# Selective scan: the input term dt·x·B made by TensorE in PSUM, decays in SBUF, D·x added by VectorE

## The chip, the cores and the metric

The kernel runs on one core of a Trainium2 chip. The metric is the device time of one launch in microseconds (us); smaller is better. A core has five engines that matter here: TensorE (PE; its weight loads are listed apart, as PEld), VectorE (DVE), ScalarE (ACT), GpSimd (POOL) and SyncE (SP, which issues the DMAs). Each runs its own list of instructions in order and waits on counting semaphores.

## The reference, cut to what matters

The kernel is a small network of several layers: a Mamba block (norm, input projection, convolution, selective scan, output projection), a layer of experts, a second mixer, and a gated feed-forward layer. The change lies in the selective scan of the first block. For each of 4 sequences of 256 tokens, 1024 channels d and 16 states n it computes

```python
def step(h, inp):                      # h: [batch, d, n], one step per token
    x_t, dt_t, B_t, C_t = inp
    dA = jnp.exp(dt_t[..., None] * A)                              # decay
    dBx = dt_t[..., None] * B_t[:, None, :] * x_t[..., None]       # input term
    h = dA * h + dBx
    y = jnp.einsum('bdn,bn->bd', h, C_t)
    return (h, y)
# and afterwards  y = y + x * D
```

## The kernel before

The stages run one behind the other, each in a block of its own that starts when all engines have left the one before. Three concern us. `scan_front` makes x (tile `xc`), dt and the rows of B and C (`sp_bcn`, 64 rows of 1024 tokens); it writes B and C to DRAM as `bc_rows`, and ends with VectorE adding the two parts of dt (L530). `selective_scan` is the stage that is changed. `scan_out_proj` multiplies the result by the output weights. Later, the norm stage `n1_` loads x again and then the weights of the experts, both from SP's queue.

In `selective_scan` channels lie on the 128 partitions (8 tiles of 128) and tokens along the row. The work is cut into 8 blocks, one for each pair of channel tiles (PR = 4) in each half of the tokens (HALF = 512, so 2 sequences); a block is a row of 2 x 512 = 1024 elements per partition. Each block has 16 units, one for each state n: 128 units in all. The `half` loop is a Python loop, the loop over the pairs is a hardware loop (`Fori`) on each engine. A unit is:

- ScalarE makes the decay exp(A·dt) into PSUM, two instructions of 510 columns (L657, tile `ss_da`, two buffers). The first token of each sequence has decay zero, so one scan can run over several sequences.
- The input term `ss_dbx` = u·B, with u = dt·x (L709, in PSUM) and B's row broadcast over the partitions (`ss_bc`), is one product of 1024 elements: on VectorE for three states of four (L703), on GpSimd for the fourth (L752, `ss_dbp`, from a copy `ss_us` of u in SBUF that ScalarE makes, L665).
- VectorE scans: h = decay·h + input (L726, out to one of four slices of tile `o`).
- GpSimd multiplies h by the broadcast row of C (L757, `ss_pr`, two buffers).
- TensorE adds that product into PSUM, `ss_y`: two f32 matmuls of 512 columns with the identity as weights (L775). At a block's start it has put D·x there, with the diagonal of D as weights (L768, `ss_dg` made by ScalarE at L669).
- At a block's end ScalarE copies `ss_y` over `xc` (L680).

The order on VectorE is: input term of unit n+1, then scan of unit n. TensorE waits for GpSimd's product, GpSimd for VectorE's scan, and ScalarE's next decay for the scan that frees its buffer:

```python
if n + 1 < NST:
    if not by_pool(n + 1):
        inputs(k, n + 1)
```

Of the kernel before, what the change touches and what calls it, by code (L numbers as in the profile page):

```python
# [21 lines left out]
P = 128  # L22
# [60 lines left out]
def build(nc, I, out):  # L83

    with ExitStack() as top:
        sems = {}

        def sem(name):
            if name not in sems:
                sems[name] = top.enter_context(nc.semaphore(name))  # L90
            return sems[name]

# [11 lines left out]
        bc_dram = nc.dram_tensor("bc_rows", [2 * NST, TOK], F32, kind="Internal").ap()  # L104
# [12 lines left out]
        def norm_stage(tag, x, o, load_x, xT, rms, keep, weights=None):  # L117
# [3 lines left out]
            with scope() as c:  # L121
# [24 lines left out]

                with nc.Block() as block:
# [126 lines left out]
                    def _(pe):  # L274
                        if xT is None:
                            return
                        for m in range(MT):
# [3 lines left out]
                            i.then_inc(s_t, 1)  # L281

# [14 lines left out]
        with scope() as c0:  # L297
            o = sb(c0, "o1", [P, MT, DM])
            with scope() as c1:
                xc = sb(c1, "xc", [P, CD, TOK])  # L300
                sz = sb(c1, "sz", [P, CD, TOK])
                with scope() as cdt:
                    dt = sb(cdt, "dt", [P, CD, TOK])
                    with scope() as c2:
# [4 lines left out]
                        scan_front(nc, sem, sb, banks, I, xT, xc, sz, dt, cst, eps, bc_dram, o)  # L309
                    selective_scan(nc, sem, sb, banks, I, xc, dt, o, ident, bc_dram)  # L310
# [25 lines left out]
def scan_front(nc, sem, sb, banks, I, xT, xc, sz, dt, cst, eps, bc_dram, o):  # L336
# [5 lines left out]
    with ExitStack() as c:  # L342
# [23 lines left out]
        s_sd, s_bcn, s_out = sem("sp_sd"), sem("sp_normed"), sem("sp_bc_out")  # L366
# [9 lines left out]
        with nc.Block() as block:  # L376
            @block.sync
            def _(sp):
# [13 lines left out]
                sp.dma_start(bc_dram, bcn[RNK:R, :]).then_inc(s_out, 16)  # L392
# [14 lines left out]
            def _(pe):  # L407
# [59 lines left out]
                for i in range(done, NT):  # L467
                    steps(i)

            @block.vector  # L470
            def _(dve):
# [59 lines left out]
                dve.wait_ge(s_dt, CD)  # L531
# [40 lines left out]
def selective_scan(nc, sem, sb, banks, I, xc, dt, o, ident, bc_dram):  # L572

    DA, RH = 2, 4
    PR = CD // 2
    W = 2 * HALF
    with ExitStack() as c:
        bcb = sb(c, "ss_bc", [P, 2 * NST, HALF])
        al = sb(c, "ss_al", [P, CD, NST])
        na = sb(c, "ss_na", [P, CD, NST])  # L580
        dd = sb(c, "ss_d", [P, CD])
        dg = sb(c, "ss_dg", [P, 2, P])
        dbx = [sb(c, f"ss_dbx{i}", [P, 2, HALF]) for i in range(2)]
        us = sb(c, "ss_us", [P, 2, HALF])
        dbp = [sb(c, f"ss_dbp{i}", [P, 2, HALF]) for i in range(2)]
        hv = o[:].rearrange("p (i m) d -> p i (m d)", i=RH)
        hh = [hv[:, i, :] for i in range(RH)]
        pr = [sb(c, f"ss_pr{i}", [P, 2, HALF]) for i in range(2)]
        wide = lambda name: c.enter_context(nc.psum_tensor(name, [P, W], F32))
        da = [wide(f"ss_da{i}") for i in range(DA)]  # L590
        u, yb = wide("ss_u"), wide("ss_y")
        s_in = sem("ss_in")
        s_bc = [sem(f"ss_bc_in{i}") for i in range(NST // 4)]
        s_a, s_z, s_da, s_u, s_dbx, s_h = (sem("ss_a"), sem("ss_zero"), sem("ss_decay"), sem("ss_u_ready"),
                                           sem("ss_dbx_ready"), sem("ss_h_ready"))
        s_pr, s_y, s_dg, s_fin = sem("ss_prod"), sem("ss_summed"), sem("ss_diag"), sem("ss_done")
        s_us, s_dbp = sem("ss_u_copied"), sem("ss_dbx_by_pool")
        UH = PR * NST
        BR = 4
        NV = NST // BR * (BR - 1)  # L600
        NP = NST // BR
        two = lambda t: t.rearrange("p (a t) -> p a t", a=2)

        def row(n):
            return bcb[:, n, :].unsqueeze(1).to_broadcast([P, 2, HALF])

        def by_pool(n):
            return n % BR == BR - 1

        def v_count(n):  # L610
            return n // BR * (BR - 1) + n % BR

        def rows_landed(eng, half, n):

            if n % BR == 0:
                eng.wait_ge(s_bc[n // BR], 32 * (half + 1))

        def tiles(eng, body):

            with eng.Fori(0, PR - 1) as k:  # L620
                body(k, False)
            body(PR - 1, True)

        with nc.Block() as block:
            @block.sync
            def _(sp):
                sp.dma_start(al[:], I["a_log0"]).then_inc(s_in, 16)
                sp.dma_start(dd[:], I["d_0"]).then_inc(s_in, 16)
                for half in range(NH):
                    for r0 in range(0, NST, BR):  # L630
                        if half:
                            sp.wait_ge(s_dbx, PR * NV - NV + v_count(r0 + BR))
                            sp.wait_ge(s_dbp, PR * NP - NP + (r0 + BR) // BR)
                        for r in (r0, NST + r0):
                            if half and r >= NST:
                                sp.wait_ge(s_pr, RH + UH - NST + r0 + BR)
                            src = bc_dram[r:r + BR, half * HALF:(half + 1) * HALF]
                            sp.dma_start(bcb[:, r:r + BR, :], src.partition_broadcast(P)).then_inc(s_bc[r0 // BR], 16)

            @block.scalar  # L640
            def _(act):
                act.wait_ge(s_in, 32)
                act.activation(al[:], al[:], ACT.Exp).then_inc(s_a, 1)
                act.wait_ge(s_a, 1)
                act.activation(na[:], al[:], ACT.Copy, scale=-1.0).then_inc(s_a, 1)
                act.wait_ge(s_a, 2)
                act.wait_ge(s_z, DA)
                for half in range(NH):
# [1609 lines left out]
```

## Time and profile before

| | |
|---|---|
| median of 3 runs | 2677.43 us |
| lowest, highest | 2675.04, 2677.46 us |
| span of the profiled execution | 2670.2 us |
| TensorE busy | 2308.2 us (86%) |
| VectorE busy | 1957.9 us (73%) |
| ScalarE busy | 1460.8 us (55%) |
| GpSimd busy | 1238.2 us (46%) |

The profile is of one execution. Times in it are counted from the start of its span. The span leaves out what lies around the instructions (about 7 us here). The profile gives for each engine the busy share in 40 slices of the span, groups of equal instructions with their mean duration, the idle time before them and what ended it, and a timeline. Matmuls overlap each other, so the duration of one (592 ns) is longer than the distance from one start to the next; for TensorE it is the distance between starts that counts. An f32 matmul appears as two MATMUL records, each with its weight load (2 x 128 x 2 = 512 records on L775).

### The profile page before, as it was taken

The page shows a single profiled execution, that of the slowest core. Times are in us where ns is not written, and L with a number is a line of the kernel's source. Part 1 is how long each engine was busy: PE and PEld are TensorE (multiplying, and loading weights), DVE is VectorE, ACT ScalarE, POOL GpSimd, SP SyncE. Part 2 cuts the span into 40 slices and gives each one's busy share as a digit, 9 for nine tenths or more (in the row PEclk, how much of TensorE's full clock was granted, in tenths as well). Part 3 has the DMA queues.
Part 4 walks back from the last instruction along what each step waited for, and adds up shares of the span by engine and source line. Part 5 has one row for each costly group of instructions (what it writes and reads, how often), then busy time and mean ns, then how long its engine had stood idle before and what let it go on. Part 6 is the DMA issues. An engine that isn't in the chain of part 4 may idle for free. (4 is left out here: it accounts for less than half of the span.)

```text
span 2670.2 us, 33973 instructions
## 1 busy us (share of the span) xinstructions
PE 2308.2 (86%) x11172; PEld 1672.4 (63%) x11172; DVE 1957.9 (73%) x3153; ACT 1460.8 (55%) x3092; POOL 1238.2 (46%) x788
## 2 busy tenths in 40 slices
PE   5966676667454999999999999999999999779997
PEld 4532222225434677777777777777777777569996
DVE  4559989994554786686685776775866866688777
ACT  2344444443103796685785866866956857742221
POOL 2119988993101464363462553644643624542212
PEclk9989998998576999999999999999999999899999
DMA  2030030000112232231332322322312312211010
GB/s 80 26 115 13 0 126 0 0 0 32 60 36 74 90 119 66 76 115 52 90 99 57 101 76 71 111 72 74 108 67 77 113 52 88 91 45 37 36 48 32
DMA packets 113218, 175.20 MB, mean 66 GB/s; under 512 B 9696, under 2 KB 77664, under 8 KB 112032
## 3 DMA queue, kind: packets, MB, share of 16 engines
q1 hardware_dynamic: 113056, 173.16, 20.6%
q8 instruction: 87, 1.43, 0.2%
q14 instruction: 75, 0.61, 0.1%
HBM read 166.71 MB, written 6.42 MB: 65 GB/s over the span
## 5 line engine op out<-in xcount | busy, mean ns | idle before, releaser
L78 PE MATMUL mg_pb<-xTh,mg_wh 128*128 128x512 f32 x1152 | 479.2, 416 | 16.9 <-POOL mg_wl L1233 16.9
L1243 POOL TENSOR_TENSOR mg_y<-mg_hT,mg_sg 128x512 f32<-128x512 f32 x128 | 187.7, 1466 | 598.9 <-DVE mg_hT L1479 598.9
L79 PE MATMUL mg_pb<-xTl,mg_wh 128*128 128x512 f32 x1152 | 454.3, 394 | 0.0
L80 PE MATMUL mg_pb<-xTh,mg_wl 128*128 128x512 f32 x1152 | 452.1, 392 | 0.0
L775 PE MATMUL ss_y<-ss_pr,cst 128*128 128x512 f32 x512 | 278.5, 678 | 125.7 <-POOL ss_pr L757 125.4
L1427 DVE SCALAR_TENSOR_TENSOR mg_hT<-mg_pb,mg_cw,mg_hT 128x510 f32<-128x510 f32 (+2 forms) x432 | 318.4, 741 | 31.6 <-ACT mg_hT L1599 22.8
L757 POOL TENSOR_TENSOR ss_pr<-o,ss_bc 128x1024 f32<-128x1024 f32 x128 | 301.9, 2374 | 45.9 <-DVE o L726 26.9
L1454 DVE TENSOR_TENSOR mg_m<-mg_gb,mg_cb 128x384 f32<-128x384 f32 x512 | 265.3, 549 | 71.6 <-ACT mg_gb L1649 68.2
L775 PEld LDWEIGHTS ss_y<-ss_pr,cst 128*128 128x128 f32 x512 | 98.4, 210 | 305.6 <-POOL ss_pr L757 225.8
L657 ACT ACTIVATE ss_da<-dt,ss_na 128x510 f32 (+1 forms) x256 | 165.9, 680 | 208.0 <-DVE o L726 208.0
L78 PEld LDWEIGHTS mg_pb<-xTh,mg_wh 128*128 128x128 f32 x1152 | 217.2, 189 | 76.5 <-issue 19.2
L80 PEld LDWEIGHTS mg_pb<-xTh,mg_wl 128*128 128x128 f32 x1152 | 217.3, 189 | 51.1
L79 PEld LDWEIGHTS mg_pb<-xTl,mg_wh 128*128 128x128 f32 x1152 | 217.9, 189 | 38.4
L1649 ACT ACTIVATE mg_gb<-mg_nd 128x256 f32<-128x256 f32 x512 | 189.6, 370 | 54.4 <-DVE mg_nd L1472 54.4
L726 DVE TENSOR_TENSOR_SCAN o<-ss_da,ss_dbx 128x1024 f32<-128x1024 f32 x96 | 215.6, 2273 | 0.0
L1643 ACT ACTIVATE mg_gb<-mg_abc,mg_tabs 128x128 f32<-128x128 f32 x512 | 183.0, 357 | 23.1 <-DVE mg_m L1454 22.1
L1233 POOL TENSOR_TENSOR mg_wl<-mg_ws,mg_wh 128x1024 fp32r<-128x1024 f32 x72 | 177.5, 2465 | 6.0
L78 PE MATMUL mg_tb<-mg_wogh,mg_yh 128*128 128x512 f32 x448 | 179.9, 401 | 0.0
L80 PE MATMUL mg_tb<-mg_wogh,mg_yl 128*128 128x512 f32 x448 | 177.0, 395 | 0.0
L79 PE MATMUL mg_tb<-mg_wogl,mg_yh 128*128 128x512 f32 x448 | 176.9, 395 | 0.0
L1329 PE MATMUL mg_py<-mg_m,mg_hc 128*64 128x256 f32 x1024 | 166.1, 403 | 9.6 <-DVE mg_m L1454 9.5
L1503 DVE SCALAR_TENSOR_TENSOR o<-mg_tb,mg_rs,o 128x512 f32<-128x512 f32 x56 | 41.8, 746 | 179.7 <-PE mg_tb L80 179.7
(289 smaller groups left out, 5217.4 us busy)
## 6 DMA issues: line engine op xcount, KB each, us to landing
mg_abc<-acs_rows SPq DMA_DIRECT2D x256, 256.0 KB, 3.4
mg_ws<-in_w_in SPq DMA_DIRECT2D x72, 512.0 KB, 3.8
ss_bc<-bc_rows SPq DMA_DIRECT2D x16, 1024.0 KB, 6.4
mg_wos<-in_w_out SPq DMA_DIRECT2D x64, 256.0 KB, 3.6
ff_ws<-in_w SPq DMA_DIRECT2D x7, 1024.0 KB, 4.7
x<-in_x SPq DMA_DIRECT2D x16, 256.0 KB, 4.1
ip_ws<-in_w_in SPq DMA_DIRECT2D x8, 512.0 KB, 3.6
ff_w2s<-in_w SPq DMA_DIRECT2D x7, 512.0 KB, 5.7
```

The costliest lines, as they stand in the source:

```text
L78: pe.matmul(out, lhs[0], rhs[0], start=start, stop=False)
L79: pe.matmul(out, lhs[0], rhs[1], start=False, stop=False)
L80: return pe.matmul(out, lhs[1], rhs[0], start=False, stop=stop)
L726: dve.tensor_tensor_scan(hh[n % RH], da[n % DA][:], src[:].rearrange("p a t -> p (a t)"), 0.0, ALU.mult, ALU.add).then_inc(s_h, 1)
L757: pool.tensor_tensor(pr[n % 2][:], two(hh[n % RH]), row(NST + n), ALU.mult).then_inc(s_pr, 1)
L775: i = pe.matmul(yb[:, a * HALF:(a + 1) * HALF], ident, pr[n % 2][:, a, :], start=False, stop=n == NST - 1)
L1233: pool.tensor_tensor(wl[s % 2][:], ws[:], wh[s % 2][:].bitcast(F32), ALU.subtract).then_inc(s_lo, 1)
L1243: pool.tensor_tensor(yb[:, p % RING, t], hT[s % 2][:, t], sg[s % 2][:, t], ALU.mult).then_inc(s_y2, 1)
L1427: i = dve.scalar_tensor_tensor(out=d3, in0=s3, scalar=w[:, TAPS - 1 - k:TAPS - k], in1=d3, op0=ALU.mult, op1=ALU.add)
L1454: dve.tensor_tensor(mm[u % 4][:], gb[u % 2][:, 0:BLK], cbt[:, u // 2, :], ALU.mult).then_inc(s_m, 1)
L1643: act.activation(gb[u % 2][:, 2 * P:BLK], abc[(BATCH * p + b) % 3][:, hh, P:SEQ], ACT.Exp, bias=tabs[g % 2][:, 2, 2 * b, 2 * q + hh:2 * q ...
L1649: act.activation(gb[u % 2][:, 0:2 * P], nd[u % 4][:], ACT.Exp, scale=1.0 if by_dve(p, b) else -1.0).then_inc(s_e, 1)
```

## The change

The input term moves from VectorE and GpSimd to TensorE. For a matmul that gives u[d, t]·B[t, n] with channels on the output partitions, u is turned: per block TensorE transposes the eight 128x128 pieces of u into PSUM (`turn`), ScalarE copies them to SBUF as `ss_uT` (`copied`), and then per unit TensorE runs eight f32 matmuls of 128x128 by 128 columns (`inputs`): weights are a piece of `ss_uT`, the moving operand is a diagonal matrix of B for that state and those 128 tokens (`ss_diag`). The result goes to `ss_dbx`, now in PSUM with two buffers; the decays go to SBUF. The diagonals are made once per half: for the first by VectorE (states 0 to 3), GpSimd (4 to 9) and ScalarE (10 to 15), for the second by ScalarE during the last block of the first half. For this `scan_front` turns the B rows with eight transposes and a copy into a small tile `bt`, ahead of VectorE's last additions. Only C's rows go through DRAM and are broadcast.

u is made in SBUF by VectorE. The D·x term is no longer a matmul: at the end of a block VectorE computes xc = D·xc + sum (`skip`, two instructions of 512). PSUM tile `z` (two buffers) holds first the turned u and then the block's sum. `ss_pr` has three buffers instead of two. All loops over blocks are unrolled. TensorE's order in step i is: input term of unit i+2, then (after unit 8 of a block) the turn for the next block, then the sum of unit i-2.

Since the unrolled waits need no offsets but semaphores run short, `n1_` clears the semaphores of the three stages on SP between its load of x and its load of weights, for use again.

```diff
+                        if tag == "n1_":
+                            cleared.extend(clear_stages(sp, "ip_", "sp_", "ss_"))
...
+                for m in range(MT):
+                    i = pe.transpose(pq[:, m * R:(m + 1) * R], bcn[:, m * P:(m + 1) * P], cst[0:R, C_ID:C_ID + R])
+                i.then_inc(s_bt, 1)
...
+                dve.wait_ge(s_bt, 1)
+                dve.tensor_copy(bt[:], pq[:].rearrange("p (m r) -> p m r", r=R)[:, :, RNK:RNK + NST]).then_inc(s_dt, 1)
...
+    RH, RP, LEAD, LAG = 4, 3, 2, 2
+    TURN_AT, EVAC_AT = 8, 4
...
+                def decay(i):
+                    kk, n = divmod(i, NST)
+                    if i >= 2:
+                        act.wait_ge(s_h, i - 1)
+                    for a in range(2):
...
+                        ins = act.activation(out[:, :, 1:], src[:, :, 1:], ACT.Exp, scale=na[:, k, n:n + 1])
+                    ins.then_inc(s_da, 1)
+                def copied(kk):
+                    act.wait_ge(s_ut, kk + 1)
+                    if kk:
+                        act.wait_ge(s_dbx, kk * NST)
+                    for a in range(2):
+                        act.activation(uT[:, a].rearrange("p m d -> p (m d)"), z[kk % 2][:, a * HALF:(a + 1) * HALF],
+                                       ACT.Copy).then_inc(s_us, 1)
+                def narrow_diag(half, n):
+                    for m in range(TB):
+                        ins = act.activation(diag[:, n, m, :], ident, ACT.Copy,
+                                             scale=bt[:, half * TB + m, n:n + 1])
+                    ins.then_inc(s_dact, 1)
...
+                def scan(i):
+                    dve.wait_ge(s_da, i + 1)
+                    dve.wait_ge(s_dbx, i + 1)
+                    if i >= RH:
+                        dve.wait_ge(s_pr, i - RH + 1)
+                    dve.tensor_tensor_scan(hh[i % RH], da[i % 2][:], dbx[i % 2][:], 0.0, ALU.mult, ALU.add
+                                           ).then_inc(s_h, 1)
+                def skip(kk):
+                    dve.wait_ge(s_y, (kk + 1) * NST)
+                    for a in range(2):
...
+                        dve.scalar_tensor_tensor(out=xv, in0=xv, scalar=dd[:, k:k + 1],
+                                                 in1=z[kk % 2][:, a * HALF:(a + 1) * HALF], op0=ALU.mult, op1=ALU.add
+                                                 ).then_inc(s_fin, 1)
...
+                for i in range(UNITS):
+                    kk, n = divmod(i, NST)
+                    pool.wait_ge(s_h, i + 1)
...
+                    if i >= RP:
+                        pool.wait_ge(s_y, i - RP + 1)
+                    pool.tensor_tensor(pr[i % RP][:], two(hh[i % RH]),
+                                       crow[:, n, :].unsqueeze(1).to_broadcast([P, 2, HALF]), ALU.mult
+                                       ).then_inc(s_pr, 1)
...
+                def inputs(i):
+                    kk, n = divmod(i, NST)
+                    if i >= 2:
+                        pe.wait_ge(s_h, i - 1)
...
+                    for a in range(2):
+                        if n == 0:
+                            pe.wait_ge(s_us, 2 * kk + a + 1)
+                        for m in range(TB):
+                            ins = pe.matmul(dbx[i % 2][:, a * HALF + m * P:a * HALF + (m + 1) * P], uT[:, a, m, :],
+                                            diag[:, n, m, :], start=True, stop=True)
+                    ins.then_inc(s_dbx, 1)
+                def summed(i):
+                    kk, n = divmod(i, NST)
+                    pe.wait_ge(s_pr, i + 1)
...
+                    for a in range(2):
+                        ins = pe.matmul(z[kk % 2][:, a * HALF:(a + 1) * HALF], ident, pr[i % RP][:, a, :],
+                                        start=n == 0, stop=n == NST - 1)
+                    ins.then_inc(s_y, 1)
+                turn(0)
+                for i in range(LEAD):
+                    inputs(i)
+                for i in range(UNITS + LAG):
+                    kk, n = divmod(i, NST)
+                    if i + LEAD < UNITS:
+                        inputs(i + LEAD)
+                    if n == TURN_AT and kk + 1 < KB:
+                        turn(kk + 1)
+                    if LAG <= i:
+                        summed(i - LAG)
```

## Rows read from the trace of the kernel before

**Rows 1.** The page: busy tenths in 40 slices of the span (66.8 us each).
```profile
PE   5966676667454999999999999999999999779997
DVE  4559989994554786686685776775866866688777
PEclk9989998998576999999999999999999999899999
```

**Rows 2.** Busy time by stretch: PE, PEld, DVE, ACT, POOL, PEclk, DMA share, GB/s.
```profile
174.00:184.00 10.00, 3.78 (x4) 1.18 (x4) 1.33 (x2) 5.51 (x10) 0.09 (x1) 0.65 0.84 267
184.00:600.00 416.00, 282.09 (x524) 99.72 (x524) 406.23 (x229) 179.66 (x278) 366.75 (x157) 0.92 0.11 34
```

**Rows 3.** Groups from 174 to 612: line, operation | busy us, mean ns | idle before.
```profile
L757 POOL TENSOR_TENSOR ss_pr<-o,ss_bc 128x1024 f32<-128x1024 f32 x128 | 301.9, 2374 | 45.9 <-DVE o L726 26.9 <-PE ss_y L775 18.6 <-issue 0.3
L775 PE MATMUL ss_y<-ss_pr,cst 128*128 128x512 f32 x512 | 278.5, 678 | 125.7 <-POOL ss_pr L757 125.4
L726 DVE TENSOR_TENSOR_SCAN o<-ss_da,ss_dbx 128x1024 f32<-128x1024 f32 x96 | 215.6, 2273 | 0.0
L703 DVE TENSOR_TENSOR ss_dbx<-ss_u,ss_bc 128x1024 f32<-128x1024 f32 x96 | 116.8, 1223 | 16.7 <-DMA ss_bc<-bc_rows 7.0 <-ACT ss_us L665 6.8
L752 POOL TENSOR_TENSOR ss_dbp<-ss_us,ss_bc 128x1024 f32<-128x1024 f32 x32 | 75.2, 2351 | 54.2 <-DMA ss_bc<-bc_rows 49.4 <-ACT ss_us L665 4.8
L657 ACT ACTIVATE ss_da<-dt,ss_na 128x510 f32 x192 | 124.6, 680 | 163.0 <-DVE o L726 163.0
L709 DVE TENSOR_TENSOR ss_u<-dt,xc 128x1024 f32 x6 | 11.4, 1896 | 0.0
L665 ACT ACTIVATE ss_us<-ss_u 128x1024 f32<-128x1024 f32 x8 | 8.2, 1020 | 2.4 <-DVE ss_u L709 2.4
L669 ACT ACTIVATE ss_dg<-cst,ss_d 128x128 f32<-128x128 f32 x16 | 5.5, 391 | 0.0
```

**Rows 4.** The scans: duration ns min/median/max, first and last start.
```profile
L726 DVE TENSOR_TENSOR_SCAN o<-ss_da,ss_dbx x96: 2261/2278/2281, 186.2 to 600.5; 128x1024 f32<-128x1024 f32 x96
L726 DVE TENSOR_TENSOR_SCAN o<-ss_da,ss_dbp x32: 2264/2278/2281, 195.3 to 602.6; 128x1024 f32<-128x1024 f32 x32
```

**Rows 5.** Timeline, one sum of TensorE near 301: start us, us, engine.
```profile
300.54 1.98 PE L775 MATMUL ss_y<-ss_pr,cst 128*128 128x512 f32 x4 [0.33 <-POOL ss_pr L757]
301.07 0.19 PEld L775 LDWEIGHTS ss_y<-ss_pr,cst 128*128 128x128 f32 x1 [0.24 <-issue]
301.50 0.19 PEld L775 LDWEIGHTS ss_y<-ss_pr,cst 128*128 128x128 f32 x1 [0.24 <-issue]
```

**Rows 6.** Timeline near 874: f32 matmuls of 256 and 128 columns, each with weights.
```profile
873.22 0.41 PEld L1347 LDWEIGHTS mg_gb<-mg_sg,mg_hT 128*128 128x128 f32 x2
873.45 0.59 PE L1347 MATMUL mg_gb<-mg_sg,mg_hT 128*128 128x256 f32 x2
873.88 0.38 PE L1348 MATMUL mg_gb<-mg_sg,mg_hT 128*128 128x128 f32 x2
874.10 0.60 PE L1347 MATMUL mg_py<-mg_sg,mg_hT 128*128 128x256 f32 x2
```

**Rows 7.** Timeline, weight loads alone: sixteen in a row before one-column matmuls.
```profile
1024.15 1.99 PEld L1355 LDWEIGHTS mg_gb<-cst,mg_ssq 128*128 128x128 f32 x16
```

**Rows 8.** Timeline, matmuls of 512 columns in fp32r, one record each.
```profile
161.78 0.39 PE L78 MATMUL ip_pb<-xTh,ip_wh 128*128 128x512 f32 x1
162.01 0.39 PE L79 MATMUL ip_pb<-xTl,ip_wh 128*128 128x512 f32 x1
```

**Rows 9.** Timeline, start and end of the stage and the transposes at 18.
```profile
18.30 6.44 PE L280 MATMUL n_tb<-cst,n_h 128*128 128x128 f32 x32 [18.30 <-DVE n_h L196]
163.34 0.69 DVE L489 COPY sz<-ip_pb 128x512 f32<-128x512 f32 x1 [2.03 <-PE ip_pb L80]
175.70 1.23 DVE L709 TENSOR_TENSOR ss_u<-dt,xc 128x1024 f32<-128x1024 f32 x1 [1.83 <-DMA ss_d<-in_d]
611.26 1.02 ACT L680 ACTIVATE xc<-ss_y 128x1024 f32<-128x1024 f32 x1 [9.38 <-PE ss_y L775]
```

**Rows 10.** A VectorE instruction like the added one, and the weights in `n1_`.
```profile
L1503 DVE SCALAR_TENSOR_TENSOR o<-mg_tb,mg_rs,o x56: 737/749/752, 1029.6 to 2239.2; 128x512 f32<-128x512 f32 x56
685.23 2.85 POOL L174 TENSOR_SCALAR ex_wh<-ex_ws 128x650 fp32r<-128x650 f32 x4 [33.78 <-DMA ex_ws<-in_w_ex]
716.73 0.35 PE L78 MATMUL ex_pb<-ex_wh,xTh 128*128 128x138 f32 x1 [2.14 <-PEq L147]
```

More of the change, by code:

```diff
@@ L85, in build, with clear_stages @@
     with ExitStack() as top:
-        sems = {}
+        sems, spare = {}, []
         def sem(name):
             if name not in sems:
-                sems[name] = top.enter_context(nc.semaphore(name))
+                sems[name] = spare.pop() if spare else top.enter_context(nc.semaphore(name))
             return sems[name]
+        def clear_stages(sp, *starts):
+            done = [n for n in sems if n.startswith(starts)]
+            for n in done:
+                sp.sem_clear(sems[n])
+            return [sems.pop(n) for n in done]
         def scope():
@@ L580, in selective_scan @@
         na = sb(c, "ss_na", [P, CD, NST])
         dd = sb(c, "ss_d", [P, CD])
[L582 to L585, printed above, removed]
+        u = sb(c, "ss_u", [P, 2, HALF])
+        uT = sb(c, "ss_uT", [P, 2, TB, P])
+        da = [sb(c, f"ss_da{i}", [P, W]) for i in range(2)]
         hv = o[:].rearrange("p (i m) d -> p i (m d)", i=RH)
@@ L613, in rows_landed @@
[L613 to L622, printed above, removed]
+        dbx = [wide(f"ss_dbx{i}") for i in range(2)]
+        z = [wide(f"ss_z{i}") for i in range(2)]
+        s_in, s_a, s_z = sem("ss_in"), sem("ss_a"), sem("ss_zero")
+        s_c = [sem(f"ss_c_in{i}") for i in range(NST // BR)]
@@ L631, in _ @@
                         if half:
[L632 to L638, printed above, removed]
+                            sp.wait_ge(s_pr, UNITS // NH - NST + r0 + BR)
+                        src = c_dram[r0:r0 + BR, half * HALF:(half + 1) * HALF]
+                        sp.dma_start(crow[:, r0:r0 + BR, :], src.partition_broadcast(P)).then_inc(s_c[r0 // BR], 16)
             @block.scalar
@@ new lines, in _ @@
+                copied(0)
+                decay(0)
+                decay(1)
+                for n in range(P_FIRST, NST):
+                    narrow_diag(0, n)
+                for i in range(2, UNITS):
+                    kk, n = divmod(i, NST)
+                    decay(i)
+                    if n == NST - 1 and kk + 1 < KB:
+                        copied(kk + 1)
+                    if kk == PR - 1:
+                        act.wait_ge(s_dbx, i + 1)
+                        narrow_diag(1, n)
@@ new lines, in _ @@
+                dt_x(0)
+                for n in range(V_FIRST):
+                    wide_diag(dve, n).then_inc(s_dv, 1)
+                dve.wait_ge(s_in, 32)
+                for i in range(UNITS):
+                    kk, n = divmod(i, NST)
+                    scan(i)
+                    if n == EVAC_AT and kk:
+                        skip(kk - 1)
+                    if n == TURN_AT - 1 and kk + 1 < KB:
+                        dt_x(kk + 1)
+                skip(KB - 1)
+                dve.wait_ge(s_fin, 2 * KB)
@@ L739, in _ @@
             @block.gpsimd
             def _(pool):
[L741 to L757 removed]
+                for n in range(V_FIRST, P_FIRST):
+                    wide_diag(pool, n).then_inc(s_dp, 1)
@@ new lines, in _ @@
+                for i in range(UNITS):
+                    kk, n = divmod(i, NST)
+                    pool.wait_ge(s_h, i + 1)
+                    if n % BR == 0:
+                        pool.wait_ge(s_c[n // BR], 16 * (kk // PR + 1))
+                    if i >= RP:
[3 more added lines that the diff above has]
+                                       ).then_inc(s_pr, 1)
```

211 lines of the change are left out of this document (68 added, 143 removed).

## The prediction

> **What bounds the kernel now.** I first read the busy tenths by slice [rows 1]. The selective scan is the run from about 174 to 612 us, slices 3 to 10 of the 40; there TensorE shows sixes and sevens, while VectorE shows eights and nines. Next I read the busy time of the stage's middle [rows 2]: of 416 us VectorE is busy for 406.23, GpSimd for 366.75, TensorE's matmul rows cover 282.09 and ScalarE 179.66. VectorE is the bound, GpSimd close behind. The groups [rows 3] say what VectorE does: 128 scans of 2.28 us [rows 4] make 291.6, 96 input products of 1.223 make 117.4, and 8 products dt·x of 1.2 to 1.9 make about 14, in all 423. The distance from one scan to the next is (602.6 - 186.2) / 127 = 3.28 us [rows 4]. That is what a unit costs now, and the number that the change has to beat on every engine.
>
> TensorE's real load cannot be read from busy time, because its records overlap. I read starts instead. A unit's sum is four records of 512 columns (two f32 matmuls, two passes each). The second weight load begins at 301.07 and the third at 301.50, one pass apart [rows 5]: 0.4275 us taken (0.43 in the rows), so a sum occupies TensorE for 4 x 0.4275 = 1.71 us. It waits for the rest of the 3.28: it was idle for 125.7 us before L775, nearly all for GpSimd [rows 3].
>
> **The change part by part.**
>
> *Removed.* VectorE loses 96 products (117 us) and GpSimd 32 of 2.35 us (75 us) [rows 3]. TensorE loses the D·x matmuls (8 x 1.7 us), ScalarE small copies. VectorE would then need 128 x 2.28, 8 x 1.9 for dt·x and 16 instructions of 0.75 for D·x (priced by L1503, the same operation and size [rows 10]): 291.8 + 15.2 + 12.0 = 319 us, or 2.49 per unit. GpSimd needs 128 x 2.36 = 302. ScalarE needs 2 x 0.68 = 1.36 per unit for the decays [rows 3], far below.
>
> *Added on TensorE.* Per unit, eight f32 matmuls of 128 columns with different weights each, so sixteen passes and sixteen weight loads. The nearest rows are L1347 and L1348, f32 as well, full 128x128 weights, new weights for every matmul [rows 6]. The two passes of 256 columns take from 873.45 to 873.88, the two of 128 columns from 873.88 to 874.10: 0.215 and 0.11 per pass. So the cost goes with the columns, about 0.108 for each 128, and an f32 matmul of 128 columns costs 0.22 us in all. A pass cannot be shorter than its weight load, and sixteen loads with almost no matmul between them show what that takes [rows 7]: (1.99 - 0.19) / 15 = 0.12 each at most. I take 0.110 a pass, since that row is the same kind of instruction. The ends are 0.107 (half of the 256-column pass) and 0.12 (the loads). The input term then costs 16 x 0.110 = 1.76 us per unit, and a unit on TensorE is 1.76 + 1.71 = 3.47 us. This is more than VectorE's 2.49, GpSimd's 2.36, and more than the 3.28 of now. TensorE becomes the bound, and what VectorE is given back is spent as idle time.
>
> *Do the waits let TensorE run without a gap?* Count from the moment that the input term of unit i is complete. Its scan runs for 2.3 us. TensorE does a sum (1.71) and unit i+1's input (1.76), then another sum, and only at 5.2 us does it need the end of scan i, for unit i+2. The slack is 2.9 us. That covers a dt·x of 1.9 or two additions of D·x (1.5) behind a scan on VectorE. GpSimd's product starts when the scan is done and a buffer of three is free, at 5.2, and ends at 7.6; TensorE wants it at 13.9 less 1.8. So neither wait stops it. At a block's change the turned u has to be copied between the last input term of the old block and the first of the new; a sum of 1.71 us lies between, and ScalarE's copy of 1024 columns takes 1.02 in one instruction [rows 3], some 1.3 in two. I take 0, the bound is 7 x 0.3 = 2 us. The diagonals of the second half cost ScalarE four instructions of at most 0.39 [rows 3], 1.6 with 1.36 of decays, 2.9 a unit: below 3.47. If TensorE were not the bound, that block would still fit. C's rows for the second half are asked for 12 units ahead. The product dt·x and the diagonals at the start come below.
>
> *Start.* The stage begins at 173.6. The added transposes in `scan_front` run behind the last projection matmuls, and VectorE's copy of `bt` behind its last copy at 163.34 [rows 9]; VectorE is the one that ends that stage, so the copy is on the path: 0.3 us, with a short wait 0.4. (Its bounds: 0.2 and 1.) In the stage dt·x no longer waits for a DMA, which ended at 175.70 [rows 9]: it ends at 175.6 here. Eight transposes while the clock is low cost 6.44 / 32 = 0.2 each [rows 9], 1.6; the granted clock was 0.65 in this stretch [rows 2]. A half of the copy takes an estimated 0.7 (1.02 for the whole, [rows 3]), so the first input term begins at 178.2. It takes 16 x 0.22 = 3.5 at the low level, and the first scan begins at 181.8 instead of 186.2. For the next three units scans (2.28) and the waits on them set the pace, with no sums to do: the input term of unit 4 begins behind the third scan, at about 188.9. GpSimd's six diagonals (about 1.3 each, half of 2.35 and a little) are over by 182. From 188.9 on TensorE has 124 x 1.76 = 218.2 of input terms, 128 x 1.71 = 218.9 of sums and 7 turns of 8 x 0.11 = 6.2, in sum 443.3: to 632.2. Then VectorE adds D·x, 1.5, and 0.3 of latencies: 634.0. Before, the last copy ended at 611.26 + 1.02 = 612.3 [rows 9]. The difference is +21.7 us.
>
> *Outside the stage.* `n1_` clears some fifty semaphores on SP behind the eight loads of x and ahead of the weights' load. What is queued behind is that load alone. GpSimd got those weights at 685.2 and needed 9.5 us; TensorE's first matmul with them began at 716.73 [rows 10]. This gives over 20 us of cover, so I take nothing. Without that cover it would cost a few us, once. Half of the B and C traffic goes away; the DMAs were busy for 0.11 of the middle [rows 2], so nothing comes from it. Unrolling takes away small gaps on engines that wait anyway.
>
> *The sum.* The profiled span of 2670.2 becomes 2691.9. Around it lie 7.2 us up to the median; I leave them as they are. 2677.4 + 21.7 = 2699.
>
> **The rivals.**
>
> *Faster: a pass of 128 columns is cheaper in a run than in the pair of rows 6.* In fp32r, a matmul of 512 columns follows the next by 0.23 [rows 8], that is 0.057 for 128 columns. If the diagonal matmuls ran at that pace, TensorE's unit would be 16 x 0.057 + 1.71 = 2.62, and the stage 1984 passes x 0.053 = 105 us less than forecast; 2594 us. The point from which it decides is 0.099 a pass: at 21.7 / 1984 = 0.011 below my value the two kernels are even. Against it: every f32 row in the trace has two records for a matmul and 0.43 per 512 columns, and the loads alone take 0.11 to 0.12 apiece. I give it 0.09. The Trainium skill, TensorE: Matmul & The Clock Gate, section Back-to-back issue gap, has 56 ns for 128 columns and 216 for 512 once warm. By that alone the unit would be 16 x 0.056 + 4 x 0.216 = 1.8 us, TensorE would not be the bound, and the kernel would come out about 100 us faster. The rows disagree for f32, with 0.43 for a pass of 512 columns and 0.11 for 128.
>
> *Much slower: the weight load is exposed at each change between input term and sum.* The first pass of a sum that has waited takes 301.07 - 300.54 = 0.53, 0.1 more than the next [rows 5]. Two changes per unit would give 256 x 0.105 = 27 us, 2726. For it: both groups begin with a load that carries a wait. Against: at 873.22 such a load ran under the matmul before it [rows 6], and in my count the waits are long met. 0.08.
>
> *Even:* a pass near 0.099, or a start and end that win back most of it. 0.04.
>
> **How the numbers follow.** The forecast has a chance of 0.79. Its own range: 1984 passes at 0.107 to 0.12 give -6 and +20; block changes and the start give -2 to +4. So 2691 to 2722. The stated range adds the exposed loads at its upper end, 2690 to 2728, and leaves out the faster and the even case, 0.13. A measurement of this kernel can tell 0.2%, about 5.4 us, from no change. Faster 0.09, same 0.04, slower 0.87.
>
> **What would show it.** In the changed profile, TensorE's tenths should be nines all through the stage with the granted clock near full; VectorE should idle about a quarter of it, waiting for TensorE's `ss_dbx`; scans should start 3.47 us apart; sixteen passes of an input term should span 1.76 us. Wrong are: scans 2.5 apart with TensorE waiting for GpSimd or VectorE (the faster rival), TensorE idle before each group (the slower one), or a stage whose first scan isn't near 182.

## The result

The changed kernel is slower. Its median is 2705.22 us (2699.97 to 2708.02, 4 runs) against 2676.23 for the kernel before (4 runs); the ratio is 1.0116, 95% interval 1.0101 to 1.0132. The profiled execution of the changed kernel took 2699.97 us with a span of 2698.2, 28.0 more than the span of before. 2699 was forecast for the median, so the median is 6 us above it and inside the stated range of 2690 to 2728. That the profiled execution lies within 1 us of the forecast is chance: it is the fastest of the four.

The busy tenths of the page of the changed kernel, to be laid beside [rows 1]:

```profile
PE   5979999997472999999999999999999999789997
DVE  4567677775535687586686685776776866788777
PEclk9989999998776999999999999999999999899999
```

TensorE's sixes and sevens in slices 3 to 10 have become nines, with a seven at each end, and VectorE's eights and nines sixes and sevens. The engine that bounds the stage has changed. The busy time of the stage's middle (PE, PEld, DVE, ACT, POOL, then granted clock), which answers [rows 2]:

```profile
190.00:640.00 450.00, 447.66 (x2552) 324.85 (x2552) 315.57 (x147) 191.89 (x328) 297.48 (x127) 1.00 0.03 10
```

TensorE has work for 447.66 of 450 us at its full clock. VectorE is idle for 134 of them. The groups of the page say for what, with the same columns as [rows 3]:

```profile
L710 DVE TENSOR_TENSOR_SCAN o<-ss_da,ss_dbx 128x1024 f32<-128x1024 f32 x128 | 291.7, 2284 | 131.7 <-PE ss_dbx L780 121.5
L747 POOL TENSOR_TENSOR ss_pr<-o,ss_c 128x1024 f32<-128x1024 f32 x128 | 302.1, 2360 | 153.1 <-PE ss_z L790 148.2
L780 PE MATMUL ss_dbx<-ss_diag,ss_uT 128*128 128x128 f32 x2048 | 251.9, 277 | 3.9 <-DVE o L710 3.1
L790 PE MATMUL ss_z<-ss_pr,cst 128*128 128x512 f32 x512 | 240.2, 593 | 0.0
```

Scans and products take what they took before. Both engines now wait for TensorE, 121.5 and 148.2 us, and TensorE waits for almost nothing: 3.9 us ahead of the 2048 passes of the input terms, all of it by 192.31, and 0.0 ahead of the sums. One unit on TensorE, from the timeline (start, duration):

```profile
195.92 1.95 PE L780 MATMUL ss_dbx<-ss_diag,ss_uT 128*128 128x128 f32 x16
195.92 1.75 PEld L780 LDWEIGHTS ss_dbx<-ss_diag,ss_uT 128*128 128x128 f32 x15 [0.24 <-issue]
197.70 1.88 PE L790 MATMUL ss_z<-ss_pr,cst 128*128 128x512 f32 x4
```

The input term starts at 195.92 and the sum at 197.70; the next input term starts at 199.42. So a unit is 1.78 + 1.72 = 3.50 us. The fifteen weight loads start (1.75 - 0.19) / 14 = 0.1114 us apart (0.19 is the length of the last one). Over the whole stage the scans start 3.53 us apart: the first at 182.8, the last at 631.5 (the scans' own row, below), (631.5 - 182.8) / 127 = 3.533, against 3.28 [rows 4].

```profile
L710 DVE TENSOR_TENSOR_SCAN o<-ss_da,ss_dbx x128: 2253/2287/2287, 182.8 to 631.5; 128x1024 f32<-128x1024 f32 x128
```

The end of the stage, against 612.3 from [rows 9]:

```profile
640.01 1.41 DVE L718 SCALAR_TENSOR_TENSOR xc<-xc,ss_d,ss_z 128x512 f32<-128x512 f32 x2 [6.25 <-PE ss_z L790]
```

It ends at 641.4, so the stage and what lies ahead of it hold 29.1 us of the difference, and what follows is 1.1 shorter. The whole loss lies before the end of the scan stage, 0.3 us of it ahead of the stage (its first instruction starts at 173.87 and not 173.59).

### The profile page after: what moved, and what is told of

The parts are those of the page before. It is cut to its first block and busy times, and to the rows that moved or that the text cites. A ratio compares the mean times of both kernels' runs of the same rounds, so it can differ in the third digit from the quotient of the medians.

```text
span 2698.2 us, 37048 instructions
## 1 busy us (share of the span) xinstructions
PE 2471.1 (92%) x13260; PEld 1901.5 (70%) x13260; DVE 1876.2 (70%) x3078; ACT 1478.4 (55%) x3164; POOL 1175.9 (44%) x762
## 5 line engine op out<-in xcount | busy, mean ns | idle before, releaser
L710 DVE TENSOR_TENSOR_SCAN o<-ss_da,ss_dbx 128x1024 f32<-128x1024 f32 x128 | 291.7, 2284 | 131.7 <-PE ss_dbx L780 121.5
L747 POOL TENSOR_TENSOR ss_pr<-o,ss_c 128x1024 f32<-128x1024 f32 x128 | 302.1, 2360 | 153.1 <-PE ss_z L790 148.2
L780 PEld LDWEIGHTS ss_dbx<-ss_diag,ss_uT 128*128 128x128 f32 x2048 | 250.9, 193 | 63.6 <-issue 60.1
L663 ACT ACTIVATE ss_da<-dt,ss_na 128x510 f32<-128x510 f32 x256 | 170.1, 713 | 208.7 <-DVE o L710 208.7
L780 PE MATMUL ss_dbx<-ss_diag,ss_uT 128*128 128x128 f32 x2048 | 251.9, 277 | 3.9 <-DVE o L710 3.1
L790 PE MATMUL ss_z<-ss_pr,cst 128*128 128x512 f32 x512 | 240.2, 593 | 0.0
```

The lines of the kernel that those rows point to most:

```text
L710: dve.tensor_tensor_scan(hh[i % RH], da[i % 2][:], dbx[i % 2][:], 0.0, ALU.mult, ALU.add).then_inc(s_h, 1)
L747: pool.tensor_tensor(pr[i % RP][:], two(hh[i % RH]), crow[:, n, :].unsqueeze(1).to_broadcast([P, 2, HALF]), ALU.mult).then_inc(s_pr, 1)
L780: ins = pe.matmul(dbx[i % 2][:, a * HALF + m * P:a * HALF + (m + 1) * P], uT[:, a, m, :], diag[:, n, m, :], start=True, stop=True)
L790: ins = pe.matmul(z[kk % 2][:, a * HALF:(a + 1) * HALF], ident, pr[i % RP][:, a, :], start=n == 0, stop=n == NST - 1)
```

## The experiments

Theory A is that of the prediction: TensorE bounds the changed stage by the number of its passes. Its rival, B, is that waits between scan, product and matmul form a ring that sets the pace, while TensorE's rows merely fill it. The first three experiments tell them apart. The pace named below is the distance from scan to scan, averaged over the stage; the changed kernel has 3.533.

### One matmul more on TensorE

```diff
-                        for m in range(TB):
+                        for m in [0] * (1 if a == 0 else 0) + list(range(TB)):
                             ins = pe.matmul(dbx[i % 2][...], uT[:, a, m, :],
                                             diag[:, n, m, :], start=True, stop=True)
```

> The changed kernel, with the first of the eight matmuls of each input term issued twice (same operands, same output, so nothing else changes). Theory A (TensorE is the bound, and each pass costs its weight load, 0.1115 us): a unit goes from 3.504 to 3.727 us, the stage grows by 128 x 2 x 0.1115 = 28.5 us, some 2734 us. Theory B (the pace is set by a ring of waits between scan, product and matmul, and TensorE's records only fill it): under 5 us.

Measured: 2730.49 us, 1.0227 (1.0197 to 1.0257) of the kernel before, 25 us above the changed kernel. The scans of this run:

```profile
L710 DVE TENSOR_TENSOR_SCAN o<-ss_da,ss_dbx x128: 2260/2286/2289, 183.6 to 659.5; 128x1024 f32<-128x1024 f32 x128
```

(659.5 - 183.6) / 127 = 3.747, 0.214 more than 3.533. Two passes at 0.1115 are 0.223. A matmul of 128 columns, put in where it computes nothing new, costs its full two passes in each of the 128 units. That speaks for A and against B. TensorE has no gaps there (the same columns as above; the third is VectorE):

```profile
190.00:600.00 410.00, 408.32 (x2438) 305.61 (x2437) 276.88 (x129) 170.01 (x296) 255.74 (x109) 1.00 0.04 11
```

The profile puts 111.2 us of the scans' idle time in this run down to ScalarE's decays. In the steady units that is a coincidence in time and no third bound. A decay starts when a scan ends, since it needs that scan's buffer, and belongs to the scan after the next; it merely ends together with the input term that the next scan waits for (at 304.73 and 304.72, for instance).

### More work on VectorE

```diff
+                    dve.tensor_tensor_scan(hh[i % RH][:, 0:SEQ], da[i % 2][:, 0:SEQ], dbx[i % 2][:, 0:SEQ], 0.0,
+                                           ALU.mult, ALU.add).then_inc(sem("ss_again"), 1)
+                    dve.wait_ge(sem("ss_again"), i + 1)
                     dve.tensor_tensor_scan(hh[i % RH], da[i % 2][:], dbx[i % 2][:], 0.0, ALU.mult, ALU.add
                                            ).then_inc(s_h, 1)
```

> The changed kernel, with a scan of the first 256 of 1024 columns ahead of each scan, some 0.6 us more of VectorE in each unit, with a wait between the two. Theory A: VectorE then needs 2.49 + 0.65 = 3.15 us of the 3.50 that TensorE takes, so the whole grows by under 2 us, some 2706. Theory B (scans are on the path of the ring): 128 x 0.6 = 77 us more, some 2780.

Measured: 2706.16 us, 1.0129 (1.0100 to 1.0159), within 1 us of the changed kernel's median. The added work is there, and so is the idle time that it came out of:

```profile
L710 DVE TENSOR_TENSOR_SCAN o<-ss_da,ss_dbx 128x256 f32<-128x256 f32 x128 | 87.1, 681 | 47.8 <-PE ss_dbx L783 45.6 <-ACT ss_da L663 2.1
```

87.1 us of new work on VectorE cost nothing measurable; its idle time ahead of the scans fell from 131.7 to 47.8 plus 4.4 us. So the scan has at least 0.68 us of the slack of 2.9 that the prediction counted, and a ring through VectorE is excluded.

### Half the passes

```diff
-        diag = sb(c, "ss_diag", [P, NST, TB, P])
+        diag = sb(c, "ss_diag", [P, NST, TB, P], F32R)
...
-        uT = sb(c, "ss_uT", [P, 2, TB, P])
+        uT = sb(c, "ss_uT", [P, 2, TB, P], F32R)
```

> The changed kernel, with the turned u and the diagonals stored as fp32r, so each input matmul is one pass and not two (the input term is then rounded to fp32r; nothing is left out). Theory A: eight passes at their weight load of 0.1115 make 0.89 instead of 1.78 us, TensorE's unit is 2.61, next to it VectorE's 2.5 to 2.6: the stage loses 128 x 0.89 = 114 us, some 2591. If an fp32r weight load is quicker (a pass down to 0.057), VectorE is the bound at 2.5 to 2.6 and the time some 2580 to 2590 as well; the distance between passes tells the two apart. Theory B: no change.

Measured: 2602.45 us, 0.9739 (0.9711 to 0.9767), 103 us less than the changed kernel, where 114 were expected. The weight loads of one input term, on the timeline:

```profile
401.18 0.86 PEld L780 LDWEIGHTS ss_dbx<-ss_diag,ss_uT 128*128 128x128 f32 x7 [0.24 <-issue]
```

(0.86 - 0.19) / 6 = 0.112 apart. In fp32r a pass of 128 columns still takes as long as in f32, though one of 512 columns there takes 0.23 against 0.43 [rows 8, 5]. So at 128 columns with new weights a pass costs 0.11 in either format, and at one column 0.12 at most [rows 7]. What these have in common is the weight load of 128 columns. No run here passed 128 columns over weights already loaded, so that it is the load, and not another cost of each pass, is argued; and in f32 the columns alone would take 0.43 / 4 = 0.107, too near to tell the two apart.

The scans in the middle start 2.62 apart (399.67 and 402.29), as expected from 1.72 + 0.89 = 2.61; over the stage they are 2.741 apart, so 0.12 per unit, 15 us in all, are lost elsewhere. Between 190 and 600 TensorE's weight loads waited 15.6 us for VectorE, in 11 waits. One of 4.24 is in the start; seven of 1.45 stand in the middle of a block, one for each dt·x, where VectorE puts 3.05 us of it between two scans:

```profile
210.48 3.06 DVE L702 TENSOR_TENSOR ss_u<-dt,xc 128x1024 f32<-128x1024 f32 x1
213.46 6.63 DVE L710 TENSOR_TENSOR_SCAN o<-ss_da,ss_dbx 128x1024 f32<-128x1024 f32 x3
215.78 0.97 PEld L780 LDWEIGHTS ss_dbx<-ss_diag,ss_uT 128*128 128x128 f32 x8 [1.45 <-DVE o L710]
```

With TensorE's unit down to 2.61 us the slack on the scan no longer covers a dt·x.

### More work on TensorE in the kernel before

```diff
                             pe.wait_ge(s_pr, base + (RH + n + 1))
+                            pe.matmul(yb[:, 0:HALF], zero, pr[n % 2][:, 0, :], start=False, stop=False)
```

`zero` is the tile `ss_al`, scaled by 0 after its last use.

> The kernel before, with one more f32 matmul of 512 columns in each unit's sum (weights all zero, so nothing is added to the value): 0.855 us more of TensorE per unit, four times what the extra matmul of e1_extra costs. Theory A (before, VectorE is the bound at 3.28 us a unit and TensorE needs 1.71): TensorE needs 2.57, still below 3.28, and the time stays within 3 us. Rival (TensorE's sum lies on a ring with GpSimd's two product buffers, so each part of it counts): up to 128 x 0.855 = 109 us more.

Measured: 2679.53 us, 1.0037 (1.0018 to 1.0056) of the kernel before: 7 us more for 128 x 0.855 = 109 us of added work. Its scans:

```profile
L727 DVE TENSOR_TENSOR_SCAN o<-ss_da,ss_dbx x96: 2261/2278/2292, 188.1 to 607.7; 128x1024 f32<-128x1024 f32 x96
L727 DVE TENSOR_TENSOR_SCAN o<-ss_da,ss_dbp x32: 2261/2278/2280, 197.2 to 609.9; 128x1024 f32<-128x1024 f32 x32
```

(609.9 - 188.1) / 127 = 3.321, 0.04 above 3.279. The 7 us are more than the 3 that theory A gave, but a fifteenth of the work. GpSimd's wait for TensorE (two product buffers) rose from 18.6 [rows 3] to 37.3 us, so a part of the 7 us may be the rival's ring. In the kernel before TensorE had room; in the changed one a quarter of that matmul costs 25 us.

### ScalarE's diagonals behind the first decays

```diff
                 decay(0)
                 decay(1)
-                for n in range(P_FIRST, NST):
-                    narrow_diag(0, n)
                 for i in range(2, UNITS):
                     kk, n = divmod(i, NST)
                     decay(i)
+                    if 4 <= i < 4 + NST - P_FIRST:
+                        narrow_diag(0, P_FIRST + i - 4)
```

This is about a miss of the prediction. In the changed kernel the start looks like this on the timeline:

```profile
181.59 7.12 ACT L676 ACTIVATE ss_diag<-cst,bt 128x128 f32<-128x128 f32 x24
188.60 2.56 ACT L663 ACTIVATE ss_da<-dt,ss_na 128x510 f32<-128x510 f32 x4
189.97 6.77 DVE L710 TENSOR_TENSOR_SCAN o<-ss_da,ss_dbx 128x1024 f32<-128x1024 f32 x3 [2.29 <-ACT ss_da L663]
192.31 1.86 PEld L780 LDWEIGHTS ss_dbx<-ss_diag,ss_uT 128*128 128x128 f32 x16 [2.71 <-DVE o L710]
```

ScalarE makes 24 small diagonals for 7.1 us, the third decay stands behind them, the third scan waits for it, and TensorE for that scan.

> The changed kernel, with ScalarE's 24 small diagonals of the first half moved from ahead of the third decay to behind decays 4 to 9, one state each. In the changed kernel ScalarE was busy with them for 7.1 us (181.6 to 188.7) while the scan waited for decay 2. Theory A (the late start of the steady stretch, 192.3 instead of the forecast 188.9, comes from there): the third scan moves up by some 2 us, the whole gets 2 to 3.5 us shorter, too little for the whole time to tell, but plain in the trace. Rival (the low clock and the scans set the start): the input term of unit 4 still begins near 192.

```profile
183.84 2.29 DVE L710 TENSOR_TENSOR_SCAN o<-ss_da,ss_dbx 128x1024 f32<-128x1024 f32 x1 [0.97 <-PE ss_dbx L780]
186.51 8.97 DVE L710 TENSOR_TENSOR_SCAN o<-ss_da,ss_dbx 128x1024 f32<-128x1024 f32 x4 [0.38 <-PE ss_dbx L780]
191.03 1.86 PEld L780 LDWEIGHTS ss_dbx<-ss_diag,ss_uT 128*128 128x128 f32 x16 [0.32 <-DVE o L710]
```

The four scans from the second on now follow each other without a gap, and the input term of unit 4 begins 191.03 - 183.84 = 7.2 us behind the first scan instead of 192.31 - 182.81 = 9.5: 2.3 us earlier. The whole is 2699.30 us, 1.0103 (1.0075 to 1.0131), against 2705.24, 1.0119 (1.0089 to 1.0149), for the changed kernel run again beside it.

> The changed kernel as it is, for comparison with the next ones on the same chip: 1.0116 of the kernel before.

The intervals overlap, so the whole time can't tell; the trace does.

### Input term and sum both in fp32r

```diff
-        pr = [sb(c, f"ss_pr{i}", [P, 2, HALF]) for i in range(RP)]
+        pr = [sb(c, f"ss_pr{i}", [P, 2, HALF], F32R) for i in range(RP)]
...
-                        ins = pe.matmul(z[kk % 2][:, a * HALF:(a + 1) * HALF], ident, pr[i % RP][:, a, :],
+                        ins = pe.matmul(z[kk % 2][:, a * HALF:(a + 1) * HALF], idr[:], pr[i % RP][:, a, :],
```

with the turned u and the diagonals in fp32r too, and `idr` an fp32r copy of the identity.

> The changed kernel, with turned u, diagonals, products and the identity of the sum in fp32r (input terms and products are then rounded to fp32r; nothing is left out). TensorE's unit is 8 x 0.1115 + 2 x 0.23 = 1.35 us. Theory A: TensorE is out of the way, and what is late next is VectorE, with 128 x 2.28 of scans, 16 x 0.73 of D.x and 8 x 2.9 of dt.x, 2.55 us a unit, close to the 2.61 of e3_f32r: 2590 to 2600, near e3_f32r's 2602. If GpSimd's products in fp32r take longer than 2.36 it is GpSimd. Rival (in e3_f32r TensorE was still far from the only bound, the start and end count): the same as e3_f32r or above it.

Measured: 2583.61 us, 0.9667 (0.9640 to 0.9694), below the 2590 to 2600 that were expected and 19 us under the run with the input term alone in fp32r. The pace is (518.3 - 185.3) / 127 = 2.622, 0.12 less than there, 15 us in all; the eight dt·x took 2.24 us on average and not 2.92, 5.5 less in all. The stage's middle:

```profile
190.00:500.00 310.00, 283.91 (x1232) 245.98 (x1233) 286.75 (x139) 185.44 (x324) 280.87 (x118) 0.61 0.05 18
```

VectorE is busy for 286.75 of 310 us and GpSimd for 280.87. They are nearly full, as computed, and 89 us lie between this run and the kernel before. But TensorE is not out of the way, for the granted clock is 0.61. In this stretch, for instance, it was 0.50:

```profile
228.00:243.00 15.00, 15.00 (x60) 13.84 (x60) 13.41 (x9) 8.39 (x13) 14.57 (x8) 0.50 0.01 2
231.43 2.29 DVE L712 TENSOR_TENSOR_SCAN o<-ss_da,ss_dbx 128x1024 f32<-128x1024 f32 x1 [0.27 <-PE ss_dbx L782]
231.67 2.04 PEld L782 LDWEIGHTS ss_dbx<-ss_diag,ss_uT 128*128 128x128 f32 x8
233.99 2.29 DVE L712 TENSOR_TENSOR_SCAN o<-ss_da,ss_dbx 128x1024 f32<-128x1024 f32 x1 [0.28 <-PE ss_dbx L782]
```

TensorE is busy for 15.00 of 15 us, scans start 233.99 - 231.43 = 2.56 us apart, and each waits 0.27 or 0.28 us for TensorE. At this clock TensorE's unit takes 2.56 us instead of the 1.35 expected, and it is TensorE that sets the pace.

### Another way to make the input term, in f32 throughout

With u turned, tokens lie on the partitions and B is one number per partition. ScalarE can scale the turned u by it, and TensorE turns the result back: eight transposes of one pass each, in place of eight matmuls of two.

```diff
+                def scaled(i):
...
+                    for m in range(TB):
+                        ins = act.activation(v[c % 3][:, :, m, :], uT[kk % 2][:, :, m, :], ACT.Copy,
+                                             scale=bt[:, (kk // PR) * TB + m, n:n + 1])
+                    ins.then_inc(s_v, 1)
...
+                            if by_diag(i):
+                                ins = pe.matmul(to, uT[kk % 2][:, a, m, :], diag[:, n // EV, m, :],
+                                                start=True, stop=True)
+                            else:
+                                ins = pe.transpose(to, v[scaled_before(i) % 3][:, a, m, :], ident)
```

Every fourth state keeps the diagonals, which are built by GpSimd at the start. The turned u has two buffers.

> The changed kernel, with the input term of three states of four made another way: ScalarE scales the turned u (tokens on the partitions, so B is one number per partition) with four instructions of 256 columns, and TensorE turns the result back with eight transposes, one pass each. Every fourth state keeps the diagonal. Theory A: TensorE's unit is 1.718 + (12 x 0.89 + 4 x 1.784) / 16 = 2.83 us, the stage loses 86 us against the changed kernel: some 2619, 0.979 of the kernel before. ScalarE has 1.42 + 0.75 x 4 x 0.42 = 2.7; if the four take 0.5 each it is the bound at 2.92 and the time some 2631. Theory B: no change or slower, as ScalarE joins the ring.

Measured: 2625.77 us, 0.9821 (0.9792 to 0.9850), between the 2619 of TensorE alone and the 2631 with ScalarE as the bound. The groups of the stage:

```profile
L807 PE MATMUL ss_dbx<-cst,ss_v 128*128 128x128 f32 x768 | 102.5, 278 | 9.6 <-ACT ss_v L699 4.9 <-DVE o L738 4.6
L804 PE MATMUL ss_dbx<-ss_diag,ss_uT 128*128 128x128 f32 x512 | 62.4, 275 | 0.7 <-DVE o L738 0.7
L699 ACT ACTIVATE ss_v<-ss_uT,bt 128x256 f32<-128x256 f32 x384 | 162.4, 495 | 0.0
```

Twelve of sixteen input terms are now 8 records each and not 16: 768 = 96 x 8. The pace is 2.897 against the 2.83 of TensorE's count.

The share kept on diagonals was then varied, every second state and every eighth:

> As e5_scaled, with every second state by diagonals instead of every fourth. Theory A (TensorE's passes set the pace): a unit is 1.718 + (8 x 0.89 + 8 x 1.784) / 16 = 3.06 us, 0.22 above e5_scaled's, so 28 us more than its 2626: 2654. Rival (e5_scaled is at its pace of 2.90 because ScalarE is: 1.33 + 12/16 x 1.69 = 2.60 of work and waits on top): with ScalarE at 2.18 the time would fall below 2626.

> As e5_scaled, with every eighth state by diagonals. TensorE's unit falls to 1.718 + (14 x 0.89 + 2 x 1.784) / 16 = 2.72 us, ScalarE's rises to 1.33 + 14/16 x 1.69 = 2.81. Theory A with ScalarE as the next bound: 2.81 and above, about the same as e5_scaled or a little slower, 2615 to 2640. If TensorE were still alone on the path: 14 us less, 2612.

```profile
L738 DVE TENSOR_TENSOR_SCAN o<-ss_da,ss_dbx x128: 2253/2286/2289, 188.1 to 577.6; 128x1024 f32<-128x1024 f32 x128
```

(every second), and every eighth:

```profile
L738 DVE TENSOR_TENSOR_SCAN o<-ss_da,ss_dbx x128: 2253/2286/2289, 188.6 to 544.2; 128x1024 f32<-128x1024 f32 x128
```

| states on diagonals, of 16 | TensorE's passes, us per unit | pace measured | time, us | ratio to before |
|---|---|---|---|---|
| 16 (the changed kernel) | 3.50 | 3.533 | 2705.22 | 1.0116 (1.0101 to 1.0132) |
| 8 | 3.06 | 3.067 | 2646.08 | 0.9906 (0.9889 to 0.9922) |
| 4 | 2.83 | 2.897 | 2625.77 | 0.9821 (0.9792 to 0.9850) |
| 2 | 2.72 | 2.800 | 2612.96 | 0.9762 (0.9732 to 0.9792) |

With 8 and 16 the pace is the count of passes to within 0.03 us. With 4 and 2 it stands 0.07 and 0.08 above it; ScalarE's work is then 2.60 and 2.81 per unit, and in the last case VectorE waited 17.2 us for `ss_da`, ScalarE's decays; in 300 us of its middle TensorE was busy for 295.12 and ScalarE for 289.68. It looks as if two engines share the path there; no run separated them. The forecast for 8 states was 2654, 8 us too high. For 2 states 2615 to 2640 was stated, with ScalarE as the bound, and missed by 2 us; the time is the one that TensorE alone would give (2612), the pace (2.800) nearer to ScalarE's 2.81 than to TensorE's 2.72. The last version keeps f32 throughout and is 59 us faster than the kernel before and 92 faster than the change.

## Why the prediction was right, point by point

The mechanism was right, and so was the direction. The size was off by a quarter of the effect: the medians lie 29.0 us apart where 21.7 were forecast. The stage and what lies ahead of it took 29.1 us more instead of 21.7. Of these 7.4 us 3.4 are in the start and 4.1 in the steady stretch behind it, less 0.1 for D·x at the end; each is told below.

*The bound before.* VectorE at 3.28 a unit, TensorE with 1.71 of real load: four times the added work on TensorE cost 7 us there. Right.

*The price of the input term.* 16 passes at 0.110 were taken from a row of f32 matmuls with changing weights [rows 6], with an upper end from the weight loads [rows 7]. Measured were 0.1114 to 0.1115, inside the forecast's 0.107 to 0.12. [rows 6] holds just two passes of 128 columns in a row and mixes them with passes of 256. The term that was mis-sized is this one, 1984 x 0.0015 = 3 us.

*The sum.* 1.72 against 1.71. *The unit:* 3.50 against 3.47. *The stage behind the start:* from 192.31 to D·x at 640.01 it took 447.7 us, against 443.3 and 0.3 of latency forecast. 3 of the 4.1 us are the passes of the input term, 128 x 0.01 = 1.3 the sums.

*The waits.* Forecast was that TensorE would not stop, with a slack of 2.9 us on the scan. It stopped for 3.9 us in all, each time in the start, and 0.68 us more of VectorE per unit went unnoticed. The copies at the block changes were hidden, as taken. One number under it was wrong without a cost here: dt·x takes 2.89 us on average where 1.9 was written, so VectorE needs 2.55 a unit and not 2.49.

*The start.* Here the count failed. The input term of unit 4 began at 192.3 instead of 188.9. The first scan was 1 us late: dt·x took 2.05 us and ended at 176.03, 0.4 behind the forecast, and the turn and copy of u, then the first input term, put some 0.3 each on top. (The turn was priced by the row at 18.30, taken for one at a low clock; the profile has a granted clock of 1.00 there. In the changed kernel it was 0.50, and the eight transposes took 1.97 us instead of 1.6.) 2.3 us more came from ScalarE's 24 diagonals, which the prediction priced for the second half and forgot in the first: it went through the diagonals of GpSimd at the start and never asked what stands behind ScalarE's. Moving them gave the 2.3 back.

*`scan_front`.* VectorE's copy of `bt` takes 0.29 us, and the additions behind it began at 164.22 instead of 163.95 [rows 9 has the copy ahead of both]: 0.3 as priced.

*Outside.* The semaphores' clearing holds the weights' load back by 3 us and is hidden. The last load of x was issued by 705.8 and the weights' at 708.92; GpSimd was done with them at 724.3, and the first matmul that needs them began at 745.41:

```profile
708.92 0.33 SPq L164 DMA_DIRECT2D ex_ws<-in_w_ex  x1
...
717.47 6.79 POOL L187 TENSOR_TENSOR ex_wl<-ex_ws,ex_wh 128x650 fp32r<-128x650 f32 x4
...
745.41 0.30 PE L78 MATMUL ex_pb<-ex_wh,xTh 128*128 128x138 f32 x1 [2.85 <-PEq L155]
```

*The time around the span.* 7.2 us were put around the span, and "The time and profile before" has "about 7 us". That is a misreading: in the profiled run of the changed kernel time and span are 1.8 us apart (2699.97 and 2698.2), and 1.8 to 1.9 in nearly every other execution on record. The rest is that the profiled execution of before, 2670.2 + 1.8 = 2672.0, was 5.4 us faster than the median that its span was subtracted from. The same holds of the changed kernel, 2705.22 - 2698.2 = 7.0, so the sum came to no harm, by luck.

*The rivals.* The faster one at its full size needed a pass of 0.057, and 0.099 to come out even. Even fp32r, where a pass of 512 columns is half as long, showed 0.112 at 128 columns. The Trainium skill (TensorE: Matmul & The Clock Gate, section Back-to-back issue gap) gives the 56 ns for 128 columns as the gap of an isolated matmul, and some 81 ns for a stream in which each matmul has its weight load. The prediction took the first; neither fits a row here, 111 ns in f32 and 112 in fp32r. Its section LDWEIGHTS (loading the stationary operand) puts a load at its columns divided by 1.2, in ns, which is 107 ns for 128 columns, and with 111.4 the trace agrees within 5%. The slower one needed exposed loads at each change from input term to sum; the first two loads of the sum, from 197.59 on, and its first pass at 197.70 follow the input term at the ordinary distance of 0.11.

*Not tried.* No run took the other parts of the change out one by one (D·x on VectorE, the third product buffer, the unrolled loops). With TensorE busy for 447.66 of 450 us they can't show in the time.

## What to carry to other kernels

A matmul that is cut into pieces of 128 columns, each with its own weights, costs 0.11 us per pass in f32 and in fp32r alike, about the time of its weight load, and f32 pays it twice. Before moving elementwise work onto a half-idle TensorE, count its load by the distances between starts and not by its busy time, add the new passes, and compare the sum with the pace of the engine that is to be relieved: here 1.71 + 1.78 against 3.28. Transposes are single passes, so scaling turned data by a number per partition and turning it back halves the bill if ScalarE has room (16 records for an input term became 8). And an engine that is given less to do need not leave the path: in the fp32r run TensorE's clock fell, so look at the granted clock first.

## What the runs showed of the hardware that was not expected

The granted clock fell when TensorE had less to do. With all operands in fp32r, TensorE's work at full clock is 8 x 0.1115 + 2 x 0.23 = 1.35 of the 2.62 us of a unit. The clock was 0.61 on average in the stage's middle; in the changed kernel, with 3.50 us of work in 3.53, it was 1.00. In the fp32r run some input terms took twice as long as others:

```profile
299.93 1.70 PEld L782 LDWEIGHTS ss_dbx<-ss_diag,ss_uT 128*128 128x128 f32 x8
301.87 15.40 DVE L712 TENSOR_TENSOR_SCAN o<-ss_da,ss_dbx 128x1024 f32<-128x1024 f32 x7 [1.51 <-PE ss_dbx L782]
304.21 0.97 PEld L782 LDWEIGHTS ss_dbx<-ss_diag,ss_uT 128*128 128x128 f32 x8 [1.00 <-DVE o L712]
```

The loads of the first line fall in a stretch of mostly low clock (0.61 from 299.9 to 301.6) and start about 0.21 apart, those of the last at a granted clock of 1.00 about 0.11. The scan behind the slow term waited 1.51 us for it. So part of the work that was taken off TensorE came back as a slower clock, and with it TensorE came back onto the path: VectorE waited 20.0 us for it in this stage, and from 228 to 243, at the 1.2 GHz level throughout, it set the pace.

dt·x on VectorE, both inputs in SBUF, took 1.23 us with GpSimd idle [rows 9], 1.51 to 3.08 later in the kernel before, and 3.00 to 3.02 in the changed one from the second block on. That its output lies in SBUF there is not the reason: the additions of dt on L547, all in SBUF and of the same size, take 1.22 with GpSimd idle. What decides is GpSimd's product that runs when it starts. In the changed kernel, then in the run with more work on VectorE:

```profile
320.59 2.36 POOL L747 TENSOR_TENSOR ss_pr<-o,ss_c 128x1024 f32<-128x1024 f32 x1 [1.14 <-PE ss_z L790]
321.02 3.01 DVE L702 TENSOR_TENSOR ss_u<-dt,xc 128x1024 f32<-128x1024 f32 x1
323.76 2.35 POOL L750 TENSOR_TENSOR ss_pr<-o,ss_c 128x1024 f32<-128x1024 f32 x1 [1.14 <-PE ss_z L793]
324.91 2.28 DVE L702 TENSOR_TENSOR ss_u<-dt,xc 128x1024 f32<-128x1024 f32 x1
```

The product ends at 322.95 and dt·x at 324.03; in the other run it is 326.11 and 327.19. Both times dt·x ends 1.08 us behind the product, however early it started, as if it made no headway while the product ran. In the kernel before, where its output lies in PSUM, the one at 551.16 ends 1.09 behind the product beside it. So dt·x costs what is left of GpSimd's product and 1.08 us, and its price moves with the pace of the stage.
